# A routed feed-forward block: second product in fp32 instead of three f16 products

## The chip, the cores and the metric

One core of a Trainium2 chip. The time is device microseconds of one execution of the kernel; lower is better. An engine is named as in the profile: PE (TensorE matmul), PEld (TensorE weight load), DVE (VectorE), ACT (ScalarE), POOL (GpSimd), SP (SyncE, which issues the transfers).

## What is computed

The input x is (2, 4096, 256) in fp32. Three residual blocks follow each other: feed-forward, attention, feed-forward, each on the row-wise layer norm of x. The change touches the feed-forward block alone:

```python
x_mixed = mix[0]*xp[:, :-2] + mix[1]*xp[:, 1:-1] + mix[2]*xp[:, 2:]   # neighbours in the sequence
h = einsum('bsd,pdm->bspm', x_mixed, W1) + b1                         # 9 paths, 64 inner values each
stacked = einsum('bspm,pmd->bspd', h, W2) + b2
scores = tanh(x_mixed @ Wo1 + bo1) @ Wo2 + bo2
weights = one_hot(argmax(scores), 9)                                  # one path per row
collapsed = einsum('bspd,bsp->bsd', stacked, weights)
out = layernorm(x + collapsed, gamma, beta)
x = x + 0.5 * out
```

The reference computes in fp32. The attention block (causal, softmax over absolute scores) is the same in both kernels.

## The kernel before

It is one program with five engine streams written out by hand, each in its own order; semaphores tie them together. The phases are `ffn(0)`, `attention(0)`, `attention(1)`, `ffn(1)`.

A feed-forward phase runs over 16 tiles of 512 rows (4 groups of 128 rows). It is a software pipeline in turns: `over_turns` calls `turn(t)` on each engine for t from -5 to 16. In turn t the hidden product works on tile t+1, the second product on tile t, the mixing on tile t+2, the transposes on tile t+4, the final norm on tile t-1. Turns 1 to 10 are a hardware loop, the others are written out.

The inner layer is held as 640 columns = 5 chunks of 128 (`HC`): 64 for the one-hot selection of `b2` and the tanh branch, 9 x 64 for the paths. For a tile t the steps are:

- TensorE `hidden(t, c)`, c = 0 to 4: h of one chunk, 128 x 512, as a `split_product` (L1354 to L1362). A split product takes both operands as a high and a low f16 half and makes three matmuls, high by high, high by low, low by high. Here there are two contraction halves, so 6 matmuls of 512 columns.
- ScalarE `hidden` (L1134): adds the bias, writes `hb` in fp32.
- TensorE `route` (L1423), VectorE `route` steps 0 to 4, TensorE `choice` (L1430, transposes of the one-hot), ScalarE `one_hot` (L1139): which path each row takes.
- TensorE `mask(t, c)` (L1439) spreads the one-hot over the chunk's 128 inner rows; VectorE `masked(t, c)` (L811) multiplies `hb` by it and writes `hm` in fp32, two buffers in turn.
- ScalarE `masked_high` (L1143) casts `hm` to f16 (`hhi`); VectorE `masked_low` (L816) writes the rest, `hm - hhi`, as f16 (`hlo`).
- TensorE `path(t, c)` (L1442): the chunk times W2, accumulated over the 5 chunks in `ps_o`. For each of the 4 row groups it is a split product: the 128 x 128 piece of `hhi` or `hlo` is the stationary operand, `w2_hi` or `w2_lo` of 256 columns the moving one; 12 matmuls a chunk. c = 0 waits for `y_done` (the buffer `ps_o` read by VectorE).
- VectorE `result` (L775) adds the normalised row, then statistics (`result_sums` L696, `row_moments` L703); GpSimd `norm_scale` (L529 to L541) makes scale and shift; ScalarE `normal` (L1150) applies them; GpSimd `result` (L549, L553) multiplies by gamma and adds the residual, and L564 prepares the next tile's residual plus beta.

The steps of other tiles that stand between them are: ScalarE `normalised` (L1087), the layer norm of the rows of tile t+4; TensorE `transposed` (L1368) and ScalarE `transposed` (L1094), its transposes and their copies; ScalarE `middle` (L1115), VectorE `mixed_before` and `mixed_behind` (L750, L757), the mixing; ScalarE `x_high` (L1121) and VectorE `mixed_low` (L765), the f16 halves of the mixed rows, on which `hidden(t, 0)` of the next turn waits (`xlo_done`).

In one turn the order on TensorE is hidden 0, mask 2, hidden 1, path 0, mask 3, route, hidden 2, path 1, mask 4, hidden 3, path 2, transposed 0, choice, hidden 4, path 3, transposed 1, mask 0 and 1 of the next tile, path 4. On ScalarE: hidden 0 and 1, masked_high 2, middle, masked_high 3, hidden 2, normalised, normal, masked_high 4, hidden 3, one_hot, transposed 0, x_high, hidden 4, transposed 1, masked_high 0 and 1 of the next tile, keep (L1108). On VectorE: result, masked 2, masked_low 1, result_sums, masked 3, row_moments, masked_low 2, route and mixing in turns, masked 4, masked_low 3, input_sums, masked_low 4, input_moments, mixed_low, masked 0 and 1 and masked_low 0 of the next tile. In the first phase `fold_biases` (L656 to L666) stands in VectorE's turn 14.

Before the first turns `prepare_first` and `prepare_second` on VectorE scale the weights by 64 and split them into halves.

Of the kernel before, what the change touches and what calls it, by code (L numbers as in the profile page):

```python
# [18 lines left out]
HC = (DM + NP * DM) // P  # L19
# [5 lines left out]
WS = 64.0  # L25
# [6 lines left out]
AHEAD = 5  # L32
# [5 lines left out]
def macaron(nc, x, Wq, bq, Wk, bk, Wv, bv, Wo, bo, mix, W1, b1, W2, b2, Wo1, bo1, Wo2, bo2,  # L38
# [10 lines left out]
    with ctx:  # L49
        def sb(name, shape, dt=F32):  # L50
            return ctx.enter_context(nc.sbuf_tensor(name, shape, dt))

        def sem(name):
            return ctx.enter_context(nc.semaphore(name))

        def cols(a, at, n):
            return a[:, bass.ds(at, n)]
# [20 lines left out]
        f1, f2 = Region(R1), Region(R2)  # L78
# [4 lines left out]
        hb = f2.take(HC * TT)  # L83
        hm = f2.take(2 * TT)
        hhi = f2.take(HC * TT, F16)
        hlo = f2.take(HC * TT, F16)
        xa = f2.take(DC * TT)
# [11 lines left out]
        w2_s = f1.take(HC * D)  # L99
# [31 lines left out]
        w1_lo = sb("w1_lo", [P, DC, HC * P], F16)  # L131
        w2_hi = sb("w2_hi", [P, HC, D], F16)
        w2_lo = sb("w2_lo", [P, HC, D], F16)
        wqk_hi = sb("wqk_hi", [P, DC, D], F16)
# [32 lines left out]
        ps_h, ps_m, ps_o, ps_n = PS[:, 0:2, :], PS[:, 2:4, :], PS[:, 4:6, :], PS[:, 6, :]  # L167
# [27 lines left out]
        ohT_psum, ohT_done, mask_psum = sem("ohT_psum"), sem("ohT_done"), sem("mask_psum")  # L195
        hm_done, hhi_done, hlo_done = sem("hm_done"), sem("hhi_done"), sem("hlo_done")
        o_psum, y_done, xb_done, x1_done, stored = (sem("o_psum"), sem("y_done"), sem("xb_done"), sem("x1_done"),
# [83 lines left out]
        def is_int(j, value):  # L281
            return isinstance(j, int) and j == value
# [341 lines left out]
        def _(dve):  # L624
            v = nc.vector
# [17 lines left out]
            def prepare_second():  # L643

                w2h, w2l = (w[:, :, :].rearrange("p a b -> p (a b)") for w in (w2_hi, w2_lo))
                v.tensor_scalar(w2h, w2_s, WS, None, ALU.mult).then_inc(fold_step, 1)
                v.tensor_scalar(gamma_b[:, :], gamma_b[:, :], 0.5, None, ALU.mult)
                v.tensor_scalar(beta_b[:, :], beta_b[:, :], 0.5, None, ALU.mult)
                dve.wait_ge(fold_step, 2)
                v.scalar_tensor_tensor(out=w2l, in0=w2_s, scalar=WS, in1=w2h, op0=ALU.mult, op1=ALU.subtract)\  # L650
                    .then_inc(weights_ready, 1)

# [60 lines left out]
            def ffn(ph):  # L713
# [54 lines left out]
                def result(t):  # L768

                    dve.wait_ge(o_psum, g0 + t + 1)  # L770
                    dve.wait_ge(n_kept, g0 + t + 1)
                    if not is_int(t, 0):
                        dve.wait_ge(z_done, g0 + t)
                    for i in range(2):
                        v.scalar_tensor_tensor(out=cols(y, i * TT, TT), in0=ps_o[:, i, :], scalar=1.0 / (XS * WS),  # L775
                                               in1=cols(N, slot(t) * SUB * D + i * TT, TT), op0=ALU.mult, op1=ALU.add)\
                            .then_inc(y_done, 1)
# [26 lines left out]
                def masked(t, c):  # L804

                    k = HC * (g0 + t) + c
                    dve.wait_ge(hb_done, k + 3)
                    if c >= 2 or not is_int(t, 0):
                        dve.wait_ge(hlo_done, k if c == 0 else k - 1)
                    dve.wait_ge(mask_psum, k + 1)  # L810
                    v.tensor_tensor(cols(hm, (c % 2) * TT, TT), ps_m[:, c % 2, :], cols(hb, c * TT, TT), ALU.mult)\  # L811
                        .then_inc(hm_done, 1)

                def masked_low(t, c):
                    dve.wait_ge(hhi_done, HC * (g0 + t) + c + 1)
                    v.tensor_tensor(cols(hlo, c * TT, TT), cols(hm, (c % 2) * TT, TT), cols(hhi, c * TT, TT),  # L816
                                    ALU.subtract).then_inc(hlo_done, 1)

                def turn(t):
# [10 lines left out]
                    if second:  # L830
                        masked(t, 2)
                        masked_low(t, 1)
                    if normal:
# [3 lines left out]
                    if normal:  # L837
                        row_moments(0, r_stat, r_var, g0 + t)
                    if second:
                        masked_low(t, 2)  # L840

# [9 lines left out]
                    if second:  # L851
                        masked(t, 4)
                        masked_low(t, 3)
                    if rows:
                        input_sums(t + AHEAD)
                    elif first_of(ph, t):
                        first_stats(0, first_of(ph, t))
                    if second:
                        masked_low(t, 4)
                    if rows:  # L860
# [3 lines left out]
                    if choice:  # L864
                        masked(t + 1, 0)
                        masked(t + 1, 1)
                        masked_low(t + 1, 0)

# [197 lines left out]
        def _(act):  # L1066
# [6 lines left out]
            def ffn(ph):  # L1073
# [66 lines left out]

                def masked_high(t, c):
                    act.wait_ge(hm_done, HC * (g0 + t) + c + 3)
                    a.activation(cols(hhi, c * TT, TT), cols(hm, (c % 2) * TT, TT), ACT.Copy).then_inc(hhi_done, 1)  # L1143

                def normal(t):
# [8 lines left out]
                def turn(t):  # L1154
# [18 lines left out]
                    if is_tile(t - 1) and not is_int(t, NTT):  # L1173
                        normal(t - 1)
                    if second:
                        masked_high(t, 4)
                    if first:
# [8 lines left out]
                    if is_tile(t + 4):  # L1186
                        transposed(t + 4, 1)
                    if first:
                        masked_high(t + 1, 0)
                        masked_high(t + 1, 1)  # L1190
                    if is_tile(t + 4):
# [159 lines left out]
        def _(pe):  # L1351
# [44 lines left out]
            def ffn(ph):  # L1396
# [45 lines left out]
                def path(t, c):  # L1442

                    if c == 0:
                        pe.wait_ge(y_done, 2 * (g0 + t) + 2)
                    pe.wait_ge(hlo_done, HC * (g0 + t) + c + 1)
                    for u in range(SUB):
                        at = c * TT + u * P
                        ins = split_product(ps_o[:, u // 2, (u % 2) * D:(u % 2 + 1) * D],
                                            [((cols(hhi, at, P), cols(hlo, at, P)), (w2_hi[:, c, :], w2_lo[:, c, :]))],  # L1450
                                            c == 0 and u % 2 == 0, c == HC - 1, skip=True)
                    if c == HC - 1:
                        ins.then_inc(o_psum, 1)

# [244 lines left out]
```

## Time and profile before

| | us |
|---|---|
| median of 3 runs | 1644.85 (1644.08 to 1645.97) |
| span of the profiled execution | 1643.8 |
| PE busy | 1443.9 (88%) |
| PEld busy | 784.2 (48%) |
| DVE busy | 1325.6 (81%) |
| ACT busy | 1049.0 (64%) |
| POOL busy | 472.3 (29%) |

The first feed-forward phase lasts to about 392 us of the span, attention from there to about 1264 us, the last phase to the end. A busy share is an average over phases with different limits; where an engine's idle time ends, and on whom it waited, is read in the timeline. Matmuls are pipelined: the duration of one reaches into the next, so the cost of one in a stream is the distance between two starts. An fp32 matmul stands in the trace as two records. "PEclk" is the TensorE clock that was granted, as a share of 2.4 GHz.

### The profile page before, as it was taken

Reading aid. Unit: us, or ns where it says so; the run is one execution under the profiler, and the core shown is the slowest. Engines: PE = TensorE matmul, PEld = TensorE weight load, DVE = VectorE, ACT = ScalarE, POOL = GpSimd, SP = SyncE. Lnnn points to the kernel's source line nnn. Section 1 sums busy time; section 2 is a strip of 40 time slices with the busy share of each in tenths; the row PEclk is TensorE's granted clock in tenths of the full one; section 3 lists DMA queues with packets and bytes.
Section 4 is the critical chain, followed back from the end, with each engine's and each line's share of the span. In section 5 each row is a group of like instructions: output and inputs, shape, how many; then the busy total and the mean of one; then the engine's idle time right before and its main releaser. Section 6 shows DMA issues by size and latency. Waiting matters only on the chain.

```text
span 1643.8 us, 29203 instructions
## 1 busy us (share of the span) xinstructions
PE 1443.9 (88%) x7860; PEld 784.2 (48%) x7860; DVE 1325.6 (81%) x2580; ACT 1049.0 (64%) x1879; POOL 472.3 (29%) x488
## 2 busy tenths in 40 slices
PE   4988888877999999999978999999988888988885
PEld 2555454444445544545344444545444455544443
DVE  5999999997677776777866777777788799999985
ACT  5767666644666676676755676666666677776652
POOL 3355556655110100000040110000001166555544
PEclk9999899988999999999989999999999899899987
DMA  6011111111001100002010101001031011011001
GB/s 168 27 39 38 51 51 51 52 39 52 1 27 39 39 0 26 16 23 82 22 41 1 39 27 39 24 2 39 0 103 42 10 52 51 26 51 38 27 26 39
DMA packets 66361, 62.47 MB, mean 38 GB/s; under 512 B 6939, under 2 KB 66276, under 8 KB 66276
## 3 DMA queue, kind: packets, MB, share of 16 engines
q1 hardware_dynamic: 66276, 61.44, 12.0%
q8 instruction: 41, 0.67, 0.2%
q14 instruction: 44, 0.36, 0.1%
HBM read 36.26 MB, written 25.17 MB: 37 GB/s over the span
## 4 chain that ended last, share of the span: by engine, by line
PE 60%; DVE 14%; ACT 10%; issue 10%; POOL 2%; ACTq 1%; DVEq 1%; SPq 1%; DMA 0%; POOLq 0%
PE PS L1360 52%; DVE R L765 5%; PE PS L1550 3%; ACT R L1087 2%; ACT R L1150 2%; PE PS L1439 2%; PE PS L1423 2%; DVE st L696 1%; ACT R L1245 1%; DVE R L948 1%; ACT R L1249 1%; DVE R L816 1%; ACT R L1143 1%; PE PS L1368 1%; ACT R L1121 1%
## 5 line engine op out<-in xcount | busy, mean ns | idle before, releaser
L1360 PE MATMUL PS<-R 128*128 128x512 f16 (+3 forms) x3456 | 715.2, 362 | 29.2 <-DVE R L948 17.4
L1360 PEld LDWEIGHTS PS<-R 128*128 128x128 f16 (+1 forms) x3456 | 326.3, 98 | 395.3 <-issue 34.6
L1360 PE MATMUL PS<-R,w_hi 128*128 (+1 forms) x640 | 216.5, 424 | 97.2 <-DVE R L765 97.2
L529 POOL TENSOR_SCALAR veps<-mv 128x4 f32<-128x4 f32 x80 | 30.9, 387 | 866.7 <-DVE mv L703 854.8
L948 DVE TENSOR_TENSOR R<-R 128x512 f16<-128x512 f32 (+3 forms) x288 | 188.8, 656 | 112.1 <-ACT R L1249 110.8
L1236 ACT ACTIVATE R<-PS 128x512 f32 (+5 forms) x288 | 160.2, 558 | 168.9 <-PE PS L1360 168.4
L1360 PE MATMUL PS<-w_hi,R 128*128 128x256 f16 x1280 | 243.7, 278 | 17.2 <-DVE R L816 12.7
L1245 ACT ACTIVATE R<-R 128x512 f32 (+4 forms) x288 | 169.6, 589 | 47.3 <-DVE R L942 46.6
L1143 ACT ACTIVATE R<-R 128x512 f16<-128x512 f32 x160 | 98.9, 624 | 157.8 <-DVE R L811 157.5
L942 DVE TENSOR_TENSOR R<-R,max_row 128x512 f32 (+4 forms) x288 | 187.4, 651 | 7.7 <-ACT max_row L1283 7.7
L1249 ACT ACTIVATE R<-R 128x512 f16<-128x512 f32 (+3 forms) x288 | 171.3, 595 | 27.0 <-PE PS L1360 0.8
L936 DVE TENSOR_TENSOR run_max<-run_max,R 128x512 f32<-128x512 f32 (+3 forms) x272 | 174.1, 640 | 9.3 <-DVE run_max L936 1.7
L1360 PE MATMUL PS<-w_lo,R 128*128 128x256 f16 x640 | 177.9, 278 | 0.0
L816 DVE TENSOR_TENSOR R<-R 128x512 f16<-128x512 f32 x160 | 163.3, 1020 | 15.7 <-ACT R L1143 12.6
L1360 PEld LDWEIGHTS PS<-w_hi,R 128*128 128x128 f16 x1280 | 127.7, 100 | 66.4 <-issue 16.8
L765 DVE TENSOR_TENSOR R<-R 128x512 f32 (+1 forms) x64 | 147.1, 2336 | 5.5 <-ACT R L1121 5.3
L1360 PEld LDWEIGHTS PS<-R,w_hi 128*128 128x128 f16 x640 | 58.0, 107 | 175.4 <-issue 98.3
L1134 ACT ACTIVATE R<-PS,b1c 128x512 f32<-128x512 f32 (+1 forms) x160 | 108.5, 678 | 50.1 <-PE PS L1360 48.9
L1360 PE MATMUL PS<-R,w_lo 128*128 (+1 forms) x320 | 135.2, 423 | 0.0
L811 DVE TENSOR_TENSOR R<-PS,R 128x512 f32<-128x512 f32 x160 | 106.6, 682 | 30.3 <-PE PS L1439 29.5
L696 DVE BATCH_NORM_STATS2 st<-R 128x6 f32<-128x256 f32 (+1 forms) x320 | 111.6, 410 | 3.4 <-DMA R<-in_L_attn_x 2.4
L532 POOL TENSOR_TENSOR rstd<-veps,half 128x4 f32<-128x4 f32 x80 | 97.9, 1224 | 6.7
(110 smaller groups left out, 1722.7 us busy)
## 6 DMA issues: line engine op xcount, KB each, us to landing
R<-x_scratch SPq DMA_DIRECT2D x48, 512.0 KB, 4.1
x_scratch<-R SPq DMA_DIRECT2D x32, 512.0 KB, 3.1
R<-in_L_attn_x SPq DMA_DIRECT2D x16, 512.0 KB, 4.4
out<-R SPq DMA_DIRECT2D x16, 512.0 KB, 3.1
R<-in_L_ffn_W SPq DMA_DIRECT2D x2, 288.0 KB
R<-in_L_ffn_W SPq DMA_DIRECT2D x1, 512.0 KB
R<-in_L_attn_Wq SPq DMA_DIRECT2D x1, 256.0 KB, 4.0
R<-in_L_attn_Wk SPq DMA_DIRECT2D x1, 256.0 KB, 4.5
```

Source lines behind the costliest of these rows:

```text
L696: ins = v.bn_stats(st[:, i, u, :], cols(src, at + u * D, D))
L765: v.tensor_tensor(cols(xlo, at, TT), cols(xm, c * TT, TT), cols(xhi, at, TT), ALU.subtract).then_inc(xlo_done, 1)
L816: v.tensor_tensor(cols(hlo, c * TT, TT), cols(hm, (c % 2) * TT, TT), cols(hhi, c * TT, TT), ALU.subtract).then_inc(hlo_done, 1)
L936: v.tensor_tensor(run_max[:, lo:], run_max[:, lo:], cols(ring, at, TT - lo), ALU.max)\
L942: v.tensor_tensor(cols(ring, at, TT - lo), cols(ring, at, TT - lo), max_row[:, lo:], ALU.subtract)\
L948: v.tensor_tensor(p_lo[:, i * TT + lo:(i + 1) * TT], pf[:, (i % 2) * TT + lo:(i % 2 + 1) * TT], p_hi[:, i * TT + lo:(i + 1) * TT], ALU.sub ...
L1134: a.activation(hb[rows, c * TT:(c + 1) * TT], ps_h[rows, c % 2, :], ACT.Identity, bias=b1c[rows, c:c + 1], scale=1.0 / WS).then_inc(hb_don ...
L1143: a.activation(cols(hhi, c * TT, TT), cols(hm, (c % 2) * TT, TT), ACT.Copy).then_inc(hhi_done, 1)
L1236: a.activation(cols(ring, ring_m + i * TT + lo, TT - lo), ps_s[:, i, lo:], ACT.Abs, scale=1.0 / (QS * XS * D ** 0.5)).then_inc(abs_done, 1)
L1245: a.activation(p, cols(ring, ring_n + i * TT + lo, TT - lo), ACT.Exp)\
L1249: a.activation(p_hi[:, i * TT + lo:(i + 1) * TT], p, ACT.Copy).then_inc(phi_done, 1)
L1360: ins = t_.matmul(dst, w, xx, start=start and n == 0, stop=stop and n == last, skip_group_check=skip)
```

## The change

The masked values and W2 stay in fp32; there are no halves of either. `masked_high` and `masked_low` and the buffers `hhi`, `hlo`, `w2_hi`, `w2_lo` are gone. `hm` has five chunk buffers instead of two. `path` makes one fp32 matmul per row group and chunk, 4 a chunk. Its wait is now on `hm_done`; every chunk's `path` counts in `path_psum`, on which `masked` of the next tile (same chunk buffer) and `result` wait. The first `path` of a phase also waits for `nT_done`, since one bank of `ps_o` holds transposes of the first tiles. `prepare_second` writes `w2` in one operation.

```diff
-        hm = f2.take(2 * TT)
-        hhi = f2.take(HC * TT, F16)
-        hlo = f2.take(HC * TT, F16)
+        hm = f2.take(HC * TT)
...
-        w2_hi = sb("w2_hi", [P, HC, D], F16)
-        w2_lo = sb("w2_lo", [P, HC, D], F16)
+        w2 = sb("w2", [P, HC, D])
...
             def prepare_second():
-                w2h, w2l = (w[:, :, :].rearrange("p a b -> p (a b)") for w in (w2_hi, w2_lo))
-                v.tensor_scalar(w2h, w2_s, WS, None, ALU.mult).then_inc(fold_step, 1)
                 v.tensor_scalar(gamma_b[:, :], gamma_b[:, :], 0.5, None, ALU.mult)
                 v.tensor_scalar(beta_b[:, :], beta_b[:, :], 0.5, None, ALU.mult)
+                v.tensor_scalar(w2[:, :, :].rearrange("p a b -> p (a b)"), w2_s, WS, None, ALU.mult)\
+                    .then_inc(fold_step, 1)
                 dve.wait_ge(fold_step, 2)
-                v.scalar_tensor_tensor(out=w2l, in0=w2_s, scalar=WS, in1=w2h, op0=ALU.mult, op1=ALU.subtract)\
-                    .then_inc(weights_ready, 1)
+                dve.sem_inc(weights_ready, 1)
...
                 def result(t):
-                    dve.wait_ge(o_psum, g0 + t + 1)
+                    dve.wait_ge(path_psum, HC * (g0 + t) + HC)
...
                     dve.wait_ge(hb_done, k + 3)
-                    if c >= 2 or not is_int(t, 0):
-                        dve.wait_ge(hlo_done, k if c == 0 else k - 1)
+                    if not is_int(t, 0):
+                        dve.wait_ge(path_psum, k - HC + 1)
                     dve.wait_ge(mask_psum, k + 1)
-                    v.tensor_tensor(cols(hm, (c % 2) * TT, TT), ps_m[:, c % 2, :], cols(hb, c * TT, TT), ALU.mult)\
+                    v.tensor_tensor(cols(hm, c * TT, TT), ps_m[:, c % 2, :], cols(hb, c * TT, TT), ALU.mult)\
                         .then_inc(hm_done, 1)
-                def masked_low(t, c):
-                    dve.wait_ge(hhi_done, HC * (g0 + t) + c + 1)
-                    v.tensor_tensor(cols(hlo, c * TT, TT), cols(hm, (c % 2) * TT, TT), cols(hhi, c * TT, TT),
-                                    ALU.subtract).then_inc(hlo_done, 1)
...
-                def masked_high(t, c):
-                    act.wait_ge(hm_done, HC * (g0 + t) + c + 3)
-                    a.activation(cols(hhi, c * TT, TT), cols(hm, (c % 2) * TT, TT), ACT.Copy).then_inc(hhi_done, 1)
...
                     if c == 0:
                         pe.wait_ge(y_done, 2 * (g0 + t) + 2)
-                    pe.wait_ge(hlo_done, HC * (g0 + t) + c + 1)
+                        if is_int(t, 0):
+                            pe.wait_ge(nT_done, DC * (g0 + AHEAD - 1) + 1)
+                    pe.wait_ge(hm_done, HC * (g0 + t) + c + 3)
                     for u in range(SUB):
-                        at = c * TT + u * P
-                        ins = split_product(ps_o[:, u // 2, (u % 2) * D:(u % 2 + 1) * D],
-                                            [((cols(hhi, at, P), cols(hlo, at, P)), (w2_hi[:, c, :], w2_lo[:, c, :]))],
-                                            c == 0 and u % 2 == 0, c == HC - 1, skip=True)
-                    if c == HC - 1:
-                        ins.then_inc(o_psum, 1)
+                        ins = t_.matmul(ps_o[:, u // 2, (u % 2) * D:(u % 2 + 1) * D], cols(hm, c * TT + u * P, P),
+                                        w2[:, c, :], start=c == 0 and u % 2 == 0, stop=c == HC - 1,
+                                        skip_group_check=True)
+                    ins.then_inc(path_psum, 1)
```

The calls of `masked_high` and `masked_low` in the three `turn` functions go with them.

## Rows read from the trace of the kernel before

**Rows 1.** Stretches: us, busy of PE, PEld, DVE, ACT, POOL (xinstructions), PEclk, DMA, GB/s.
```profile
145.57:163.06 17.49, 17.48 (x115) 10.73 (x115) 17.09 (x38) 15.35 (x27) 9.52 (x9) 1.00 0.08 27
...
166.76:185.65 18.89, 18.89 (x115) 11.07 (x115) 17.58 (x38) 15.24 (x27) 9.65 (x10) 0.91 0.07 24
40.30:74.77 34.47, 34.44 (x230) 21.48 (x230) 31.16 (x67) 27.29 (x49) 12.40 (x13) 1.00 0.01 2
```

**Rows 2.** Timeline of TensorE: start, us, what, xcount, [idle before <-releaser].
```profile
78.13 0.60 PE L1360 MATMUL PS<-R,w_hi 128*128 x2 [3.36 <-DVE R L765]
...
150.18 0.39 PE L1439 MATMUL PS<-oh_t,expand 9*128 9x512 f16 x1
...
157.04 0.60 PE L1368 MATMUL PS<-ident,R 128*128 128x128 f32 x4
157.57 0.39 PE L1430 MATMUL PS<-ident,oh 128*9 128x128 f16 x4
...
161.57 0.28 PE L1360 MATMUL PS<-w_hi,R 128*128 128x256 f16 x1
161.69 0.27 PE L1360 MATMUL PS<-w_lo,R 128*128 128x256 f16 x1
...
166.76 0.60 PE L1360 MATMUL PS<-R,w_hi 128*128 x2 [3.70 <-DVE R L765]
...
341.90 1.03 PE L1360 MATMUL PS<-R,w_hi 128*128 128x512 f16 x2 [3.93 <-DVE R L765]
...
1330.04 0.60 PE L1360 MATMUL PS<-R,w_hi 128*128 x2 [1.26 <-DVE R L765]
...
1594.93 1.04 PE L1360 MATMUL PS<-R,w_hi 128*128 128x512 f16 x2 [3.93 <-DVE R L765]
```

**Rows 3.** Timeline of VectorE in the turn from 145.57.
```profile
151.66 0.37 DVE L703 BATCH_NORM_AGGREGATE mv<-st 128x2 f32<-128x6 f32 x4
...
161.12 5.29 DVE L765 TENSOR_TENSOR R<-R 128x512 f32 x2
```

**Rows 4.** Timeline of ScalarE in that turn.
```profile
153.49 2.06 ACT L1087 ACTIVATE R<-R,shift,rstd 128x256 f32 x4
155.84 2.08 ACT L1150 ACTIVATE R<-R,shift,rstd 128x256 f32<-128x256 f32 x4 [0.29 <-POOL shift L541]
...
158.92 0.57 ACT L1139 ACTIVATE oh_t<-PS 9x512 f16<-9x512 f16 x1
...
159.87 1.13 ACT L1121 ACTIVATE R<-R 128x512 f32 x2
```

**Rows 5.** Timeline of GpSimd in that turn.
```profile
158.00 2.36 POOL L549 TENSOR_TENSOR R<-R,gamma_b 128x1024 f32<-128x1024 f32 x1 [2.25 <-ACT R L1150]
160.68 2.43 POOL L553 TENSOR_TENSOR R<-R 128x1024 f32 x1 [0.32 <-POOL R L549]
163.38 2.48 POOL L564 TENSOR_TENSOR R<-R,beta_b 128x1024 f32<-128x1024 f32 x1 [0.26 <-POOL R L553]
```

**Rows 6.** Timeline of TensorE in attention, and the group of its fp32 weight loads.
```profile
454.88 1.03 PE L1550 MATMUL PS<-wvo,R 128*128 128x257 f32 x4
455.74 2.75 PE L1360 MATMUL PS<-R 128*128 128x512 f16 x12
...
L1550 PEld LDWEIGHTS PS<-wvo,R 128*128 128x128 f32 x256 | 46.7, 190 | 12.7 <-ACT R L1257 2.9 <-DVE R L957 0.8 <-ACT max_row L1283 0.4
```

**Rows 7.** Page, costliest groups: busy us, mean ns, idle before.
```profile
L816 DVE TENSOR_TENSOR R<-R 128x512 f16<-128x512 f32 x160 | 163.3, 1020 | 15.7 <-ACT R L1143 12.6
```

**Rows 8.** Stretches again: in attention, and around the start of the last phase.
```profile
845.50:858.00 12.50, 10.47 (x64) 6.15 (x65) 6.29 (x15) 9.36 (x16) 7.00 (x5) 1.00 0.00 1
1266.50:1287.00 20.50, 11.81 (x41) 7.54 (x41) 14.40 (x42) 10.25 (x19) 12.11 (x25) 0.50 0.31 90
```

**Rows 9.** Timeline of VectorE at the end of the first phase.
```profile
352.82 5.93 DVE L664 TENSOR_SCALAR R<-R 128x256 f32<-128x256 f32 x6
...
368.04 1.29 DVE L775 SCALAR_TENSOR_TENSOR R<-PS,R 128x512 f32<-128x512 f32 x2 [0.92 <-PE PS L1360]
```

More of the change, by code:

```diff
@@ L195, in macaron @@
         ohT_psum, ohT_done, mask_psum = sem("ohT_psum"), sem("ohT_done"), sem("mask_psum")
-        hm_done, hhi_done, hlo_done = sem("hm_done"), sem("hhi_done"), sem("hlo_done")
+        hm_done, path_psum = sem("hm_done"), sem("path_psum")
         o_psum, y_done, xb_done, x1_done, stored = (sem("o_psum"), sem("y_done"), sem("xb_done"), sem("x1_done"),
@@ L831, in turn @@
                         masked(t, 2)
-                        masked_low(t, 1)
                     if normal:
@@ L838, in turn @@
                         row_moments(0, r_stat, r_var, g0 + t)
-                    if second:
-                        masked_low(t, 2)
                     for step in range(5):
@@ L852, in turn @@
                         masked(t, 4)
-                        masked_low(t, 3)
                     if rows:
@@ L857, in turn @@
                         first_stats(0, first_of(ph, t))
-                    if second:
-                        masked_low(t, 4)
                     if rows:
@@ L866, in turn @@
                         masked(t + 1, 1)
-                        masked_low(t + 1, 0)
                 over_turns(dve, turn)
@@ L1162, in turn @@
                         hidden(t + 1, 1)
-                    if second:
-                        masked_high(t, 2)
                     if mix:
                         middle(t + 2)
-                    if second:
-                        masked_high(t, 3)
                     if first:
@@ L1174, in turn @@
                         normal(t - 1)
-                    if second:
-                        masked_high(t, 4)
                     if first:
@@ L1187, in turn @@
                         transposed(t + 4, 1)
-                    if first:
-                        masked_high(t + 1, 0)
-                        masked_high(t + 1, 1)
                     if is_tile(t + 4):
```

## The prediction

> **What bounds the kernel now.** On the page's busy line TensorE and VectorE stand near each other, so neither can be called the bound from there. The change touches only the two feed-forward phases, so I went to one turn of them (one tile of 512 rows): the stretch table [rows 1], then each engine's order of time [rows 2 to 5]. TensorE works 17.49 us without a hole (145.57 to 163.06), then stands idle 3.70 us until VectorE's L765 (`mixed_low`, the low half of the mixed input) is done [rows 1, 2]. From turn starts in [rows 2], turns 2 to 13 take 341.90 - 78.13 = 263.77 us in the first phase and 1594.93 - 1330.04 = 264.89 us in the last, 22.0 us each. TensorE is not the bound there: its own work is 4.5 us shorter.
>
> Who makes L765 late? Call the turn's start s = 145.57. The two L765 stand as 5.29 us [rows 3], GpSimd runs L549, L553, L564 meanwhile [rows 5], and the ends interleave: L553 ends 163.11, the first L765 after it; L564 ends 165.86, the second L765 ends 166.40, TensorE starts at 166.76. A two-input SBUF operation of VectorE and a long GpSimd operation take turns: VectorE gets one slot of 0.54 us between two GpSimd operations. So the turn is a loop: TensorE up to the hidden product c=2, ScalarE L1087, L1150, GpSimd's three operations, the last L765, TensorE. L549 starts at s + 12.43, the last L765 ends 8.40 later, TensorE starts 0.36 after: 21.19 us, the whole distance. That is a turn with the clock at 2.4 GHz throughout (granted 1.00 [rows 1]). The next turn has the same TensorE work in 18.89 us at a granted 0.91: behind the idle a part of it ran at 1.2 GHz. The mean of 22.0 is the loop of 21.19 plus 0.8 to 0.9 us of clock.
>
> **The change part by part.** `path` has 5 chunks a turn. Before: 12 f16 matmuls of 256 columns a chunk, 0.11 us apart (161.57 to 161.69 [rows 2]), 1.31 us of streaming. After: 4 fp32 matmuls of 256 columns. The trace has fp32 matmuls of 257 columns at L1550: 4 records (two products of two records) take 0.86 to 0.87 us from 454.88 to 455.74 between f16 matmuls [rows 6], 0.217 us a record, 0.435 us a product. A chunk is 4 x 0.435 = 1.74 us, 0.43 us more; five chunks add 2.14 us a turn. The fp32 weight load takes 190 ns [rows 6] and fits under a record of 217 ns. Were it not hidden, a record would be 0.407 us and a chunk 3.26 us; at f16's rate 8 records would be 0.87 us. The row is of the same kind, so I take 1.74.
>
> The Trainium skill, "TensorE: Matmul & The Clock Gate", section "Weight-path perf modes", speaks against the change: the fast weight load is on only when the type is not FP32. The trace has 190 ns for the fp32 load, and shows in the same rows that it costs nothing at these widths; by the rule with loads in the open a chunk would be the 3.26 us above.
>
> Removed: 5 `masked_high` casts on ScalarE (L1143) and 5 `masked_low` on VectorE (L816, 163.3 us in all, mean 1.02 us because some wait for GpSimd [rows 7]). Neither is on the loop as such. Along the loop, with a warm clock:
> - One `path` stands before the hidden product c=2, so ScalarE's L1087 starts at 7.92 + 0.43 = 8.35 (153.49 before [rows 4]); four of its rows take 1.97, L1150 can start at 10.32.
> - L1150 also needs GpSimd's L541. VectorE's L811 for c=3 can start when the mask product of 150.18 is out (150.57, s + 5.00, now 5.43), 0.60 to the moments (L703), and 4.18 from there over GpSimd's small operations (151.66 to 155.84 [rows 3, 4]): 10.21. ScalarE is the later one by 0.1 us, so the L816 taken out before the moments help nothing.
> - L549 follows L1150's start by 2.16 us: s + 12.48, against 12.43.
> - ScalarE skips L1143, but waits for the `choice` transposes, which have three `path` before them: they end at 12.39 + 1.29 = 13.68 (157.96 before [rows 2]). L1139 and L1094 0.95 (158.92 to 159.87 [rows 4]), the first L1121 0.61: the first `mixed_low` can be asked for at 15.24, 2.76 us after L549's start. VectorE's first slot is at L549's end, 2.36. It misses by 0.4 us.
> - That slot stays empty, L553 follows at once and takes as long as L549: it ends at 4.8. VectorE 0.54; L564 2.21 more (163.11 + 0.54 to 165.86 [rows 5]); VectorE 0.54: 8.10 against 8.40. Next start: 12.48 + 8.10 + 0.36 = 20.94 us.
>
> TensorE's work is then 17.49 + 2.14 = 19.63 us and its idle 1.31 us. In [rows 8] the stretch that begins with an idle of 2.03 us (12.50 less 10.47) has 1.00 throughout, whereas the idle of 3.70 us was followed by 0.91 [rows 1]. So I take these turns as warm: 20.94 us.
>
> Turns 12 and 13 have no transposes and no L1087. There `choice` ends 0.53 earlier (157.04 to 157.57 [rows 2]), at 13.15, L1094 is gone, the first `mixed_low` is asked for at 14.23, 1.9 us after L549 (12.37). It gets the first slot and the second `mixed_low` the next, done by 18.0, below TensorE's own 17.49 - 1.06 (two transposes) + 2.14 = 18.57. TensorE bounds these two. Turns 2 to 13: 10 x 20.94 + 2 x 18.57 = 246.5 us. Gain 17.2 + 18.4 = 35.6 us.
>
> Ends. Last phase: turn 14's start to the last `path` is 35.5 us, with idles that end on L816. Afterwards `path` waits for `masked` and `result` alone: 18.6, 1.4 for `result`, five chunks 8.7, masks and waits 1.3: 30.0. Gain 5.5. First phase: VectorE's fold of the biases (5.93 us in L664) stands in turn 14 ahead of the last `masked`; the phase's end hangs on `result` at 368.04 and the moments behind it [rows 9]. Afterwards the fold ends at s + 17.3 of that turn, `masked` at 17.9, two masks and `path` at 20.3, against 26.1 (368.04 - 341.90), and about 1 us less from there to the moments: 6.8, say 7.0. Together 12.5.
>
> Against it: in turns 0 and 1 TensorE bounds (busy 34.44 of 34.47 us from 40.30 to 74.77 [rows 1]). Turn 1 of the first phase has room in its idle, turn 0 has none, so each phase pays 2.14 there, and turn 1 of the last phase, whose idle was 1.26 [rows 2], about 1.5: 5.8 us lost. At nothing: the preparation of `w2` (two operations become one, under the input of the first tiles; 1.4 us at most), the wait for `nT_done` in the first `path` (the cast that it replaces stood behind the same copy on ScalarE; up to 0.6 us, with TensorE's queue behind it), and the waits of `masked` and `result` on `path_psum` (products of the turn before). Attention is untouched.
>
> Sum: 35.6 + 12.5 - 5.8 = 42.3 us. The profiled span of 1643.8 becomes 1601.5; the median of the runs is 1644.85, 1.0 above the span, so **1602.5 us**.
>
> **The rivals.** (A) First slot caught. Were the first `mixed_low` 0.4 us earlier, or L549 later, it would finish by s + 18.5 in every turn and TensorE would bound turns 2 to 11: 10 x 2 x (20.94 - 19.63) = 26 us more, 1576 us. For it: the margin is 0.4 us in 15. Against: each term is from a row of the same turn.
> (B) The clock doesn't come back. Turns keep their 0.9 us: loop turns gain 20 x 0.27 = 5.4 us, turns 12 and 13 8.7, the ends 9.1, less 5.8: 17.4 us, 1627 us. For it: the rows show a fall behind an idle of 3.70 and none behind one of 2.03, but not what counts besides the idle's length. Against: 1.31 is below both.
> (C) Slower: fp32 passes don't hold the clock. From 1266.50 to 1287.00 TensorE was busy 11.81 of 20.50 us, largely with fp32 transposes, at 0.50 [rows 8]. Now 8.7 us of each turn are fp32. If half of TensorE's turn fell to 1.2 GHz, it would take 19.63/0.75 = 26.2 us; 28 turns x 4.1 = 115 us: 1760 us. It decides from 19.63/(1 - x/2) = 22.0, x = 22% of its time at the lower level (18% in the turn at 0.91). Against: L1550 ran at full rate, though in bursts of 0.87 us only.
> The Trainium skill, same page, section "Part 4: PE-mode transpose", holds that transposes don't count as busy for the clock in the same way; by it the row of (C) says nothing of fp32 products.
>
> **How the numbers follow.** Forecast 0.60 (its own range 1594 to 1612), A 0.12, B 0.15, C 0.05, and 0.08 for what I haven't seen. A measurement tells 0.2%, 3.3 us, from no change. Faster: 0.60 + 0.12 + 0.14 + 0.02 = 0.88; same 0.05; slower 0.07. The range takes in A and B and leaves C out: 1573 to 1633.
>
> **What would show it.** Right: `path` records 0.217 us apart; in turns 2 to 11 an idle of TensorE of about 1.3 us, still ended by L765; granted clock 1.00; turns of 20.9 us, and 18.6 us without idle in turns 12 and 13. A shows as no idle and turns of 19.6; B as shares below 1.00 behind short idles; C as long stretches at 0.50. The prediction is wrong above all if the 0.4 us margin closes, since that alone moves 26 us.

## The result and the profile after

| | before | after |
|---|---|---|
| median of the runs, us | 1644.46 (1641.66 to 1645.97, 4 runs) | 1601.17 (1600.85 to 1601.49, 4 runs) |
| ratio | | 0.974, 95% interval 0.9725 to 0.9756 |
| profiled span, us | 1643.8 | 1599.8 |
| PE / DVE / ACT busy, us | 1443.9 / 1325.6 / 1049.0 | 1466.2 / 1161.4 / 962.5 |
| granted clock, mean | 0.952 | 0.984 |

TensorE is busy 22 us more and the kernel is 43 us shorter. The forecast was 1602.5 us.

The lines moved: `path` is now L1421, `split_product` L1331, `mixed_low` L761, `masked` L807, `result` L771, `normalised` L1071, `normal` L1130, `x_high` L1105, GpSimd's three long operations L546, L550, L561, the last product of `fold_biases` L660, `row_moments` L699, `norm_scale` from L526.

From the page of after: the busy line, the clock in 40 slices, and the groups that the change made or moved (busy us, mean ns, idle before).

```profile
PE 1466.2 (92%) x7220; PEld 831.0 (52%) x7220; DVE 1161.4 (73%) x2419; ACT 962.5 (60%) x1719; POOL 453.8 (28%) x488
...
PEclk9999999999999999999989999999999799999998
...
L1421 PE MATMUL PS<-w,R 128*128 128x256 f32 x1280 | 305.5, 382 | 2.1 <-DVE R L771 2.1
L1421 PEld LDWEIGHTS PS<-w,R 128*128 128x128 f32 x1280 | 240.3, 190 | 58.6 <-issue 13.6
...
L761 DVE TENSOR_TENSOR R<-R 128x512 f32 (+1 forms) x64 | 136.5, 2171 | 91.1 <-ACT R L1105 90.9
```

The group of L816 [rows 7] has no counterpart. `path` waits for nobody but 2.1 us; L761, two a turn, still has a mean of 2.17 us, where `masked`, one read of which is from PSUM, has 0.68.

A turn of after as stretches: TensorE's work, its idle, the next whole turn, and turns 2 to 13 of the first phase (columns as in [rows 1]).

```profile
206.63:226.11 19.48, 19.48 (x95) 12.60 (x95) 14.68 (x34) 12.67 (x22) 10.82 (x10) 1.00 0.10 36
226.11:227.62 1.51, 0.00 (x0) 0.01 (x1) 1.51 (x2) 0.00 (x0) 1.34 (x3) 1.00 0.92 225
227.62:248.61 20.99, 19.48 (x95) 12.60 (x96) 16.19 (x35) 12.67 (x22) 12.17 (x12) 1.00 0.18 57
80.66:326.57 245.91, 231.65 (x1124) 149.21 (x1125) 191.07 (x410) 144.33 (x250) 145.66 (x135) 1.00 0.16 49
```

Against [rows 1 and 2] TensorE works 2.0 us more and idles 2.2 us less, and no part of the twelve turns is granted less than 1.00. They took 263.77 us before and take 245.91 now.

The timeline of TensorE: turn starts in the loop, the first without a wait, and one `path` chunk.

```profile
217.44 1.89 PE L1421 MATMUL PS<-w,R 128*128 128x256 f32 x8
219.17 0.60 PE L1339 MATMUL PS<-ident,R 128*128 128x128 f32 x4
...
227.62 0.60 PE L1331 MATMUL PS<-R,w_hi 128*128 x2 [1.51 <-DVE R L761]
...
289.70 0.39 PE L1331 MATMUL PS<-R,w_hi 128*128 128x512 f16 x1 [0.95 <-DVE R L761]
308.14 0.59 PE L1331 MATMUL PS<-R,w_hi 128*128 128x512 f16 x2
326.58 0.59 PE L1331 MATMUL PS<-R,w_hi 128*128 128x512 f16 x2
```

A chunk takes 219.17 - 217.44 = 1.73 us. Turns 12 and 13 (289.70 to 308.14 to 326.58) are 18.44 us each and have no idle.

Who still holds the loop? GpSimd, ScalarE and VectorE in the turn from 227.62, one fence each.

```profile
239.88 2.35 POOL L546 TENSOR_TENSOR R<-R,gamma_b 128x1024 f32<-128x1024 f32 x1 [2.55 <-ACT R L1130]
242.55 2.36 POOL L550 TENSOR_TENSOR R<-R 128x1024 f32 x1 [0.32 <-POOL R L546]
245.17 2.50 POOL L561 TENSOR_TENSOR R<-R,beta_b 128x1024 f32<-128x1024 f32 x1 [0.26 <-POOL R L550]
```

```profile
235.77 2.06 ACT L1071 ACTIVATE R<-R,shift,rstd 128x256 f32 x4
237.74 2.06 ACT L1130 ACTIVATE R<-R,shift,rstd 128x256 f32<-128x256 f32 x4
...
242.08 1.13 ACT L1105 ACTIVATE R<-R 128x512 f32 x2
```

```profile
243.03 5.18 DVE L761 TENSOR_TENSOR R<-R 128x512 f32 x2 [3.16 <-ACT R L1105]
```

`x_high` begins at 242.08 and its first half is there at about 242.7. L546 ended at 242.23 and L550 began at 242.55, so the first `mixed_low` came too late for the gap and waits for L550's end. The two end at 248.21, and TensorE starts at 248.61.

### The profile page after: what moved, and what is told of

Read it like the earlier page. It is cut to its first block, busy times and chain, and to the rows that moved or that the text cites. A ratio compares the mean times of both kernels' runs of the same rounds, so it can differ in the third digit from the quotient of the medians.

```text
span 1599.8 us, 27533 instructions
## 1 busy us (share of the span) xinstructions
PE 1466.2 (92%) x7220; PEld 831.0 (52%) x7220; DVE 1161.4 (73%) x2419; ACT 962.5 (60%) x1719; POOL 453.8 (28%) x488
## 4 chain that ended last, share of the span: by engine, by line
PE 70%; DVE 11%; issue 7%; ACT 7%; POOL 1%; DVEq 1%; SPq 1%; ACTq 1%; DMA 0%; POOLq 0%
PE PS L1331 48%; PE PS L1421 12%; DVE R L761 5%; PE PS L1521 3%; PE PS L1410 2%; PE PS L1394 2%; ACT R L1216 2%; ACT R L1220 2%; DVE R L926 1%; PE PS L1339 1%; DVE R L932 1%; ACT R L1105 1%; ACT R L1179 1%; SPq L362 1%; PE PS L1401 1%
## 5 line engine op out<-in xcount | busy, mean ns | idle before, releaser
L1331 PE MATMUL PS<-R 128*128 128x512 f16 (+3 forms) x3456 | 715.2, 362 | 29.3 <-DVE R L932 18.6
L1331 PEld LDWEIGHTS PS<-R 128*128 128x128 f16 (+1 forms) x3456 | 326.2, 98 | 395.5 <-issue 34.7
L1421 PE MATMUL PS<-w,R 128*128 128x256 f32 x1280 | 305.5, 382 | 2.1 <-DVE R L771 2.1
L1421 PEld LDWEIGHTS PS<-w,R 128*128 128x128 f32 x1280 | 240.3, 190 | 58.6 <-issue 13.6
L526 POOL TENSOR_SCALAR veps<-mv 128x4 f32<-128x4 f32 x80 | 25.1, 313 | 836.1 <-DVE mv L699 824.0
L1331 PE MATMUL PS<-R,w_hi 128*128 (+1 forms) x640 | 194.5, 386 | 39.7 <-DVE R L761 39.7
L761 DVE TENSOR_TENSOR R<-R 128x512 f32 (+1 forms) x64 | 136.5, 2171 | 91.1 <-ACT R L1105 90.9
L807 DVE TENSOR_TENSOR R<-PS,R 128x512 f32<-128x512 f32 x160 | 106.6, 682 | 64.8 <-PE PS L1410 64.7
L1331 PE MATMUL PS<-R,w_lo 128*128 (+1 forms) x320 | 122.8, 384 | 0.0
L1331 PEld LDWEIGHTS PS<-R,w_hi 128*128 128x128 f16 x640 | 55.2, 102 | 108.9 <-issue 49.3
L546 POOL TENSOR_TENSOR R<-R,gamma_b 128x1024 f32<-128x1024 f32 x31 | 73.1, 2358 | 74.8 <-ACT R L1130 73.3
L1339 PE MATMUL PS<-ident,R 128*128 128x128 f32 x384 | 61.6, 295 | 35.1 <-ACT R L1071 25.3
L1113 ACT ACTIVATE th<-PS,bo1c 64x512 f32<-64x512 f32 x32 | 21.8, 682 | 118.3 <-PE PS L1331 118.3
```

Of the source, the lines that this page charges most:

```text
L761: v.tensor_tensor(cols(xlo, at, TT), cols(xm, c * TT, TT), cols(xhi, at, TT), ALU.subtract).then_inc(xlo_done, 1)
L807: v.tensor_tensor(cols(hm, c * TT, TT), ps_m[:, c % 2, :], cols(hb, c * TT, TT), ALU.mult)\
L1331: ins = t_.matmul(dst, w, xx, start=start and n == 0, stop=stop and n == last, skip_group_check=skip)
L1421: ins = t_.matmul(ps_o[:, u // 2, (u % 2) * D:(u % 2 + 1) * D], cols(hm, c * TT + u * P, P), w2[:, c, :], start=c == 0 and u % 2 == 0, sto ...
```

## The experiments

To say where a kernel spends its time, I cut each trace at the tanh of ScalarE, which each turn has once. us of the profiled executions:

| kernel | span | turns 0, 1 | turns 2 to 11 | 12, 13 | turn 14 to the last phase's first work | falls of the clock / idles |
|---|---|---|---|---|---|---|
| before | 1643.8 | 38.4 + 36.2 | 221.2 + 221.7 | 43.0 + 43.7 | 939.2; end 46.1 | 20 of 26 |
| after | 1599.8 | 40.3 + 38.6 | 209.0 + 209.5 | 36.9 + 36.9 | 931.4; end 43.4 | 0 of 21 |
| e1 18 fillers | 1623.7 | 39.4 + 37.3 | 214.7 + 216.0 | 41.6 + 42.9 | 934.9; 44.8 | 9 of 25 |
| e5 34 fillers | 1622.3 | 40.3 + 38.1 | 211.8 + 214.1 | 41.0 + 41.0 | 935.4; 46.8 | 2 of 25 |
| e2 casts kept | 1621.1 | 41.0 + 38.8 | 212.1 + 212.8 | 42.5 + 41.1 | 935.5; 44.6 | 1 of 25 |
| e6 cast 4 kept | 1612.0 | 40.3 + 38.6 | 210.2 + 210.6 | 41.2 + 42.8 | 932.1; 43.7 | 1 of 25 |
| e7 casts 0 to 3 kept | 1611.9 | 40.9 + 38.8 | 210.9 + 212.3 | 36.6 + 36.6 | 938.8; 44.6 | 0 of 21 |
| e3 x_high first | 1563.5 | 38.6 + 38.6 | 193.1 + 193.1 | 36.9 + 36.9 | 932.1; 43.4 | 0 of 0 |
| e8 before, x_high first | 1637.9 | 39.6 + 36.1 | 220.3 + 220.3 | 43.9 + 41.1 | 937.8; 47.9 | 19 of 26 |
| e4 f16, no casts | 1524.2 | 35.1 + 35.3 | 179.1 + 179.9 | 34.8 + 35.1 | 928.9; 40.7 | 0 of 22 |

Two figures in a cell are the first and the last phase; "end" is from the last phase's turn 14. What lies ahead of each phase's turn 0 is left out (40.4 to 43.3 us ahead of the first). The last column counts TensorE's idles over 0.55 us ahead of turns 2 to 14 of both phases, and behind how many of them the granted clock fell before the next one.

### Is it the idle of TensorE that costs clock?

e1: the kernel before, with 18 matmuls more in each turn, into columns of a PSUM bank that nobody reads.

```diff
+                    if second and first:
+                        for _ in range(18):
+                            t_.matmul(PS[:, 7, 64:192], w1_hi[:, 0, 0:P], w1_lo[:, 0, 0:P], start=True, stop=True,
+                                      skip_group_check=True)
```

> The kernel before, with 18 small f16 matmuls of 128 columns added at the end of each feed-forward turn of TensorE, where it stands idle; they write to unused columns of bank 7 and nothing reads them. The rest is the kernel before. Theory (the turn is a loop of 21.2 us plus 0.8 us of low clock, and an idle of TensorE of about 1.5 to 2 us keeps the clock): the filler takes some 1.8 us of the idle of 3.3 to 3.7 us, the granted clock in turns 2 to 11 becomes 1.00, a turn 21.2 us, and the kernel gets faster by doing more: 24 turns x 0.8 = 19 us, about 1625 us. Rival (the gain of the change is the removed casts, the clock follows from nothing that TensorE's idle decides): no gain, 1644 us, or slower by up to 28 x 1.8 = 50 us if the filler lies on the path.

Measured: 1624.73 us (1623.76 to 1631.01), 0.9888 of before (0.986 to 0.9916). Two idles and the turns behind them, and the fillers:

```profile
182.41:185.11 2.70, 0.00 (x1) 0.01 (x1) 2.70 (x2) 0.00 (x0) 2.53 (x3) 1.00 0.75 220
185.11:206.32 21.21, 19.90 (x133) 12.28 (x133) 19.89 (x39) 15.30 (x27) 11.95 (x10) 0.92 0.12 39
205.01:207.32 2.31, 0.00 (x1) 0.00 (x1) 2.31 (x2) 0.00 (x0) 2.14 (x3) 1.00 0.91 254
207.32:228.56 21.24, 18.48 (x134) 11.82 (x134) 20.84 (x40) 15.35 (x27) 12.84 (x12) 1.00 0.16 49
...
181.24 1.17 PE L1497 MATMUL PS<-w_lo,w_hi 128*128 128x128 f16 x18
```

The same work takes 19.90 us at a granted 0.92 behind an idle of 2.70 us and 18.48 us at 1.00 behind 2.31 us. Useless matmuls made the kernel 1.1% faster. The expected total of 1625 us was hit, but not for its reason alone: the 18 fill only 1.0 us and not 1.8, so the idle fell to 2.1 to 3.0 us, about half of the falls stayed, and the loops gained 12.2 us; the rest came in turns 12 and 13 and at the ends. So I made it longer.

e5: the same with 34 fillers.

```diff
+                        for _ in range(34):
```

> As e1_filler with 34 small matmuls a turn in place of 18. In e1_filler the 18 took only 1.0 us (55 ns each), the idle was still 2.3 to 2.8 us, and 4 of the loop turns of the first phase held a stretch at 1.2 GHz. Theory (a shorter idle keeps the clock): 34 take 1.9 us, the idle becomes 1.5 to 1.8 us, no turn from 2 to 11 has a stretch below 1.00, all of them take 21.2 us, about 1619 us, 5 us less than with 18. Rival (the filler's gain came from something else than the idle's length, or is used up): the same 1624 to 1626 us as with 18.

Measured: 1625.18 us (1621.82 to 1628.77), 0.9886 (0.9859 to 0.9914): no faster than e1. A turn, and the one idle of the last phase's loop with a fall behind it:

```profile
165.39:186.58 21.19, 19.37 (x150) 12.71 (x150) 20.79 (x40) 15.35 (x27) 12.78 (x12) 1.00 0.15 47
...
1401.79:1403.76 1.97, 0.01 (x1) 0.01 (x1) 1.97 (x2) 0.00 (x0) 1.80 (x3) 1.00 0.96 265
1403.76:1408.00 4.24, 4.24 (x12) 1.36 (x13) 3.91 (x8) 3.52 (x5) 1.36 (x3) 0.60 0.27 96
```

In the loop it did what was expected: the turn is 21.19 us at 1.00, the distance read from before, and the loops are 17.0 us shorter than before (e1: 12.2). What it gained on e1 there was given back where TensorE is the bound, 0.9 + 0.8 us in turns 0 and 1, at the ends, 0.5 + 2.0 us, and 1.5 us ahead of the first phase's turn 0. The total is the one that the rival named; the step it was made for, a loop of 21.19 us while the clock holds, stood, but for the one fall shown.

### What did the product do alone, and what the casts?

e2: the changed kernel, with all ten casts of a turn put back as side work, in their old places; `path` stays fp32 and doesn't read them.

```diff
+                def masked_high(t, c):
+                    act.wait_ge(hm_done, HC * (g0 + t) + c + 3)
+                    a.activation(cols(hhi, c * TT, TT), cols(hm, c * TT, TT), ACT.Copy).then_inc(hhi_done, 1)
...
+                def masked_low(t, c):
+                    dve.wait_ge(hhi_done, HC * (g0 + t) + c + 1)
+                    if not (is_int(t, 0) and c == 0 and ph == 0):
+                        dve.wait_ge(hlo_done, HC * (g0 + t) + c)
+                    v.tensor_tensor(hlo[:, :], cols(hm, c * TT, TT), cols(hhi, c * TT, TT),
+                                    ALU.subtract).then_inc(hlo_done, 1)
```

> The changed kernel, fp32 product and all, but with the two casts a chunk put back in their old places as side work: ScalarE writes the high half, VectorE the low half, nothing reads them. Theory: the slot behind GpSimd's first long operation is taken by the last low cast again, so a turn is 12.3 + 8.40 + 0.36 = 21.1 to 21.2 us, TensorE's idle 1.7 us, the clock 1.00: 20 turns x 0.85 = 17 us less than before in the loop, turns 12 and 13 bound by the loop again (21 us), 5.8 us lost in turns 0 and 1, some won at the ends: about 1628 us. Rival (removed work on VectorE and ScalarE is what pays): all of that work is back and TensorE has 2.14 us more a turn, so 1645 us or above.

Measured: 1627.05 us (1622.80 to 1628.53), 0.9896 (0.9878 to 0.9914). Two of its turns:

```profile
165.21:186.48 21.27, 19.66 (x95) 12.52 (x96) 20.86 (x40) 15.45 (x27) 12.85 (x12) 1.00 0.16 49
186.48:207.65 21.17, 19.61 (x96) 12.52 (x96) 20.75 (x40) 15.45 (x27) 12.75 (x12) 1.00 0.15 49
```

Turns of 21.2 us, TensorE idle for 1.55 to 1.72 us ahead of turns 2 to 10, one fall. So making TensorE's product longer, with every cast still done, takes 17 us off: the product stands where TensorE would have idled, as the fillers did. (`path` no longer waits for the casts in it either; the loop turn of 21.2 us is that of before with the clock held, so in the loop that freedom is worth nothing.) The casts' removal is the other 26 us of the medians. The profiled execution of e2 is its fastest, so the table has 21 of them: 3 us in each loop, 5.6 and 4.2 us in turns 12 and 13, 4.1 and 1.2 us at the ends. The slower executions of e2 had a mean clock of 0.978 to 0.979 against 0.983.

Which of the casts? e6 keeps that of chunk 4 alone, e7 those of chunks 0 to 3; the edit is that of e2 with a list.

```diff
+KEPT = [4]
...
+                    if c not in KEPT:
+                        return
```

> The changed kernel with the two casts put back for chunk 4 alone, as side work that nothing reads; chunks 0 to 3 have none. Theory (what the casts cost in the loop is the slot behind GpSimd's L549 that the low cast of chunk 4 takes, and nothing else): turns 2 to 11 take 21.2 us as with all five put back, against 20.99 without; turns 12 and 13 lose the first slot to it and take about 21 us: within 3 us of e2_casts_kept, about 1624 us. Rival (each cast costs its own time): a fifth of the difference between e2_casts_kept (1627) and the changed kernel (1601), so about 1606 us.

Measured: 1611.51 us (1610.47 to 1613.68), 0.9798 (0.9778 to 0.9818).

> The complement of e6_cast_4_kept: the casts of chunks 0 to 3 are put back as side work, those of chunk 4 are not. Theory: the first slot is free, turns 2 to 11 take 21.0 us, turns 12 and 13 20.4 and 18.4 us as in the changed kernel: within 4 us of it, about 1603 us. Rival (each cast costs its own time): four fifths of the difference, about 1622 us.

Measured: 1613.75 us (1611.17 to 1614.99), 0.9811 (0.9789 to 0.9834).

Neither total was near an expectation. Both kernels have loop turns of 21.1 to 21.2 us, 0.1 to 0.2 above after. VectorE around GpSimd's first long operation in e6, where GpSimd's second begins at 221.77:

```profile
219.57 2.43 DVE L823 TENSOR_TENSOR hlo<-R 128x512 f16<-128x512 f32 x1 [1.02 <-ACT R L1152]
...
222.25 5.28 DVE L765 TENSOR_TENSOR R<-R 128x512 f32 x2
```

In e6 the cast takes the slot that is empty in after. In turns 12 and 13, where after has its `mixed_low` there, that costs 4.3 and 5.9 us (the second with a fall of the clock); in the other turns 0.1. In e7 turns 12 and 13 are those of after, and the price is at the first phase's end, 7.4 us. There VectorE folds the biases, in e7, in after and, beside it, GpSimd in after:

```profile
338.74 5.95 DVE L664 TENSOR_SCALAR R<-R 128x256 f32<-128x256 f32 x6
...
335.91 1.66 DVE L660 TENSOR_SCALAR R<-R 128x256 f32<-128x256 f32 x6
...
337.25 2.53 POOL L546 TENSOR_TENSOR R<-R,gamma_b 128x1024 f32<-128x1024 f32 x1 [2.25 <-ACT R L1130]
```

In after the fold is over as GpSimd's first long operation begins. In e7 the casts ahead of it in VectorE's queue push it 1.2 us back, and the last two of its six operations stand beside GpSimd's. The fold takes 5.9 us in before, e1, e2, e5, e7 and e8, and 1.7 us in after, e3, e4 and e6. That is 4.3 of the 7.4 us; the clock falls in e7 behind the wait of TensorE that follows (6.8 us at 1.2 GHz from 350.2), and not in after. In e7's loop turns `normalised` starts 0.1 to 0.2 us later in the turn than in after. I have no reason for that.

### Is it the missed slot that keeps the loop?

e3: the changed kernel with one edit, on ScalarE.

```diff
                     if first:
                         hidden(t + 1, 3)
+                    if mix:
+                        x_high(t + 2)
+                    if first:
                         one_hot(t + 1)
                     if is_tile(t + 4):
                         transposed(t + 4, 0)
-                    if mix:
-                        x_high(t + 2)
```

> The changed kernel with one order changed on ScalarE: the two x_high casts of tile t+2 stand before one_hot and transposed 0 instead of behind them. Theory (the first mixed_low misses VectorE's slot behind L546 by 0.4 us): it is asked for 1.0 to 1.2 us after L546's start instead of 2.8, gets the slot at 2.35, the second one the slot behind L550; mixed_low is done by s + 18.0, TensorE has no idle and bounds the turn at its own 19.5 us. Turns 2 to 11 of both phases gain 20.99 - 19.5 = 1.5 us each, 30 us: about 1571 us. Rival (the slots are not what the end of mixed_low hangs on, or one_hot, now 0.35 us later, binds): 1601 us, within 3 us.

Measured: 1565.19 us (1561.86 to 1565.38), 0.951 (0.9491 to 0.953). It is the fastest of the kernels here that compute all, 2.2% below after. A turn as a stretch, then GpSimd, VectorE and ScalarE in it:

```profile
173.03:192.34 19.31, 19.31 (x97) 12.61 (x95) 15.52 (x35) 12.68 (x23) 11.95 (x12) 1.00 0.17 54
...
186.58 2.35 POOL L546 TENSOR_TENSOR R<-R,gamma_b 128x1024 f32<-128x1024 f32 x1 [2.55 <-ACT R L1130]
189.25 2.44 POOL L550 TENSOR_TENSOR R<-R 128x1024 f32 x1 [0.32 <-POOL R L546]
...
187.93 4.31 DVE L761 TENSOR_TENSOR R<-R 128x512 f32 x2 [1.36 <-ACT R L1105]
...
186.97 1.14 ACT L1105 ACTIVATE R<-R 128x512 f32 x2
```

`x_high` starts 0.39 us after L546 instead of 2.20; VectorE waits from 187.93, gets the first slot and the second, and is done at 192.24. TensorE has no idle: 19.31 of 19.31 us.

e8: the same edit on the kernel before.

> The kernel before (all halves, f16 product), with nothing changed but ScalarE's x_high moved ahead of one_hot and the first transposed, the same edit that took the changed kernel to 1565 us. Theory: in the kernel before, VectorE's slot between GpSimd's L549 and L553 is held by the cast of chunk 4 (L816, 158.47 to 160.90 in the profile of before), which stands ahead of mixed_low in VectorE's queue and needs masked_high 4. So an earlier x_high isn't used: both mixed_low still end between and behind L553 and L564, the loop stays at 21.2 us, the idle of TensorE at about 3.7 us, and the time at 1644, within 6 us. The gain of the reorder then belongs to the change and the reorder together, and not to either alone. Rival: mixed_low waits for x_high also in the kernel before, the slot is used twice or GpSimd stops for less time, the turn falls to 18 to 19.5 us and the time below 1610.

Measured: 1640.82 us (1637.08 to 1646.37), 0.9977 (0.9961 to 0.9992). VectorE, ScalarE and GpSimd in a turn:

```profile
157.87 2.43 DVE L816 TENSOR_TENSOR R<-R 128x512 f16<-128x512 f32 x1 [0.21 <-ACT R L1143]
...
160.51 5.29 DVE L765 TENSOR_TENSOR R<-R 128x512 f32 x2
...
158.31 1.14 ACT L1121 ACTIVATE R<-R 128x512 f32 x2
...
157.40 2.35 POOL L549 TENSOR_TENSOR R<-R,gamma_b 128x1024 f32<-128x1024 f32 x1 [2.30 <-ACT R L1150]
160.07 2.44 POOL L553 TENSOR_TENSOR R<-R 128x1024 f32 x1 [0.32 <-POOL R L549]
```

The first half of `x_high` is there at about 158.9, 0.9 us ahead of the gap that follows L549 (159.75), and it doesn't help: L816 of chunk 4 stands in front of `mixed_low` in VectorE's queue, was asked for during L549, and holds the slot. The edit is worth 36 us after the change and 4 us before it. So the cast had to go first, as I read these rows; no run has the reorder with the cast of chunk 4 alone.

### What would the casts' removal be worth without the longer product?

e4: W2 and the masked values in f16, no cast. It leaves out the low half of the masked values: `masked` writes f16, and the three matmuls of a split product all take it, in the low half's place too, so TensorE has its old number of matmuls but the values are not those of the block.

```diff
-        hm = f2.take(HC * TT)
+        hm = f2.take(HC * TT, F16)
...
+                        part = cols(hm, c * TT + u * P, P)
+                        ins = split_product(ps_o[:, u // 2, (u % 2) * D:(u % 2 + 1) * D],
+                                            [((part, part), (w2_hi[:, c, :], w2_lo[:, c, :]))],
+                                            c == 0 and u % 2 == 0, c == HC - 1, skip=True)
```

> The changed kernel without the fp32 product: masked writes f16 once, and path makes 12 f16 matmuls of 256 columns as before, the f16 value standing for its low half as well; so the low half of the masked values is left out and the casts are away, with TensorE's work as in the kernel before (17.4 us a turn). It is the removal of the casts alone. Theory: three path chunks of 0.43 us less stand before choice, so the first mixed_low is asked for 1.9 us after L546's start and catches the first slot; turn 12.05 + 5.65 + 0.36 = 18.1 us with an idle of 0.6 us and clock 1.00. 20 turns x 3.9 = 78, turns 12 and 13 16, ends 14: about 1536 us. Rival (the short idle of the changed kernel comes only from TensorE's added work, and without it the idle of 3.3 us and the low clock stay): about 1630 us.

Measured: 1521.94 us (1518.98 to 1525.96), 0.9248 (0.9229 to 0.9267). A turn is 17.97 us with 0.67 us of idle, and the first slot is caught:

```profile
163.03 3.46 DVE L763 TENSOR_TENSOR R<-R 128x512 f32 x2 [2.37 <-ACT R L1107]
```

Both `mixed_low` end in 3.46 us instead of 5.18. With `path` 0.43 us shorter a chunk, the three of them ahead of the `choice` transposes no longer push `x_high` behind the slot, which fits the margin of 0.4 us that the forecast named (e3 shows it without touching the product). So after stands 79 us above a kernel of this shape: 36 of them are the missed slot, as e3 shows, and 43 lie between e3 and e4, where TensorE's turn is 19.31 us against 17.97. That the product earns part of this back only because the kernel before had idle time to fill is argued from e1 and e2.

## Why the prediction was right, step by step

The time came out 1.3 us under the forecast. By its own terms, cut as it cut them, where TensorE starts turns 0, 2 and 14 (40.33, 78.13, 341.90 and 1294.34, 1330.04, 1594.93 before; 40.37, 80.66, 326.58 and 1269.94, 1308.57, 1554.88 after):

| term | forecast | measured |
|---|---|---|
| turns 2 to 13 | 35.6 | 17.86 + 18.58 = 36.4 |
| first phase's turn 14 to the last phase's turn 0 | 7.0 | 9.1 |
| last phase's turn 14 to the end | 5.5 | 3.9 |
| turns 0 and 1 | -5.8 | -2.5 - 2.9 = -5.4 |
| sum | 42.3 | 44.0, as the span |

That the two ends add up is luck: one term came 2.1 us over and the other 1.6 us under, for reasons that the forecast did not have.

- **The price of the product** was right: 1.73 us a chunk (1.74), from fp32 rows of another phase. The weight load took its 190 ns and stayed hidden. A turn's work grew by 1.99 us (17.49 to 19.48) and not by 2.14. The rule of the Trainium skill, "TensorE: Matmul & The Clock Gate", section "Weight-path perf modes", that the fast weight load leaves FP32 out, cost nothing here.
- **The clock** was right, and is the largest piece. At 21.19 us ten loop turns are 211.9; before had 221.2 and 221.7, so about 19 us of the gain is clock alone. That work put where TensorE idled brings it is shown from both sides: fillers without any change of the product (e1, e5), and the product with all casts still done (e2). Rival B fell: no clock fall behind 21 idles of 0.95 to 1.58 us. Rival C fell too: of 19.48 us of work 8.7 are fp32, all at 1.00.
- **The missed slot** was right, and Rival A was what one reordering made true (e3). The forecast of A, 1576, was 11 us above e3, mostly because e3's TensorE works 19.31 us a turn and not 19.63 (6.4 us), and turns 0 and 1 gain 1.7.
- **The loop turn** was right by two errors that cancel. Forecast 20.94, measured 20.99. L546 starts at 12.26 us in the turn (239.88 - 227.62), not 12.48: `normal` starts at 10.12, not 10.32, since L1071 starts at 8.15 and not 8.35. I had added the whole longer `path` to ScalarE's step; 0.2 us of it was absorbed, where I did not find. But from L546 to the last `mixed_low` it takes 8.33 us and not 8.10. The step that failed there is "that slot stays empty, L553 follows at once": GpSimd leaves 0.32 us between the two (242.23 to 242.55) though VectorE takes nothing, as it does when VectorE is there [rows 5]. An empty slot is worth 0.1 us here (L550 takes 2.36 us, and 2.44 in e3 with a taker), not 0.3. Behind L546 the first `mixed_low` was asked for at 2.8 us (2.76).
- **Turns 12 and 13** were right: 18.44 us each (18.57) without idle. e6 shows that their gain hangs on the absent cast of chunk 4.
- **Turns 0 and 1** lost 5.4 us (5.8). The first phase paid 2.5, a little over the 2.14 of one turn. The last paid 2.9 and not 3.6: its turn 1 had an idle of 1.26 us [rows 2], which takes up that much of the longer product, and I had charged 1.5 there where 2.14 - 1.26 = 0.9 was the sum to make.
- **The first phase's end** gained 9.1 us (7.0). The step that failed is "the fold ends at s+17.3": it kept the fold's 5.93 us. The fold took 1.66 us and ended at s+11.0, since without the casts ahead of it it no longer stands beside GpSimd's long operations (e7 shows it from the other side). `result` then started at s+18.6 (345.21 - 326.58), where the forecast had `path` end at 20.3.
- **The last phase's end** gained 3.9 us (5.5). Up to `result` the forecast was right: turn 14's start to it is 1584.83 - 1554.88 = 29.95 us (30.0; 35.56 before). The failed step is that it changed nothing behind `result`. VectorE, then GpSimd, in after:

```profile
1584.83 1.29 DVE L771 SCALAR_TENSOR_TENSOR R<-PS,R 128x512 f32<-128x512 f32 x2 [4.59 <-PE PS L1421]
...
1587.70 0.38 DVE L699 BATCH_NORM_AGGREGATE mv<-st 128x2 f32<-128x6 f32 x4
...
1587.49 2.34 POOL L561 TENSOR_TENSOR R<-R,beta_b 128x1024 f32<-128x1024 f32 x1
1589.91 0.19 POOL L526 TENSOR_SCALAR veps<-mv 128x4 f32<-128x4 f32 x1
```

The moments are done at 1588.08, but GpSimd is still on the tile before until 1589.83 and starts on them at 1589.91, 1.8 us later; before it was free and started 0.2 us behind them (1633.75, 1633.94). The faster TensorE had caught up with GpSimd.

## What to carry to other kernels

An engine's longer work is free, or better than free, where it fills an idle behind which the clock fell: compare the granted clock of turns behind short and long idles before pricing it. When two engines take turns at something, list who holds each slot and who asks for it when: an edit that is worth little while the slot is held (e8, 4 us) may be the larger one once it is free (e3, 36 us). After a change that wins, ask again what is late by a few tenths of a microsecond. And a duration read from a trace (the fold's 5.93 us) can hold a wait for another engine; where the change moves either of the two, it is not a constant.

## What the runs showed of the hardware

- **VectorE beside GpSimd.** A 128x512 subtraction with both inputs in SBUF takes 0.68 us alone (median of L816 in before) and 2.43 us in before, e6 and e8, where it is asked for during a 128x1024 operation of GpSimd: in e8 that operation ends at 159.75, the subtraction at 160.30, 0.55 us behind it and 0.23 us into GpSimd's next. The Trainium skill, "GPSIMD Engine Reference", section "1. Specifications", says that the SBUF interfaces of the two are shared, with contention for VectorE's instructions with two SBUF inputs. The traces agree and show the size: the wait is to the end of GpSimd's operation, not a share of its rate. The fold's operations, with one SBUF input each, wait too: of the six of 128x256, the first four take 0.35 us each in before and the last two, beside GpSimd, 2.45 and 2.50 us. In the hardware loop GpSimd leaves 0.32 us between its first two long operations with a taker and without; in the turns written out it leaves 0.08 us.
- **fp32 matmuls.** 256 columns take 0.433 us (1.73 / 4) where an f16 matmul takes 0.109 (1.31 / 12): 4.0 times. The Trainium skill, "FP8 and Floating Point Precision", section "TensorE Precision Notes", gives true FP32 as four passes; the trace agrees in time, and shows the four as two records.
- **Small matmuls.** The fillers of 128 columns take 0.06 us each with their own weight load (1.17 us for 18, the last one's tail with it).
- **The clock.** Falls by TensorE's idle between turns: none behind 21 idles of 0.95 to 1.58 us (after) and none behind e7's 21, up to 1.61 us; one or two among 25 in e2, e5 and e6, each behind 1.97 to 2.17 us; 9 of 25 in e1, behind 2.40 to 3.02 us; 20 of 26 before, behind 3.00 to 4.02 us. But length alone doesn't decide: e5 had a fall behind 1.97 us, e1 none behind two idles of 2.92 us, and [rows 8] has 2.03 us without one. What else counts stays open.
